# Powers on GpSimd, another lane order, an earlier router chain and spare products in a two-layer network on one core

## The reference, cut to what matters

```python
# retention of layer 2, its end (stage E)
mu = jnp.mean(o, axis=-1, keepdims=True)
var = jnp.var(o, axis=-1, keepdims=True)
o = (o - mu) * jax.lax.rsqrt(var + EPS)
o = jax.nn.silu(g) * o.reshape(b, l, d)
o = o @ Wout
...
# expert layer of layer 1 (stage C)
gate_scores = jax.nn.softmax(gate_logits, axis=-1)
topk_val, topk_idx = jax.lax.top_k(gate_scores, TOP_K)
topk_val = topk_val / (topk_val.sum(axis=-1, keepdims=True) + EPS)
for e in range(E):
    a, b = jnp.split(h, 2, axis=-1)
    g = a * jax.nn.sigmoid(b)
    out = out + eo * comb[..., e:e + 1]
# expert layer of layer 2 (end of stage E)
probs = jax.nn.softmax(logits, axis=-1)
top_w, top_i = jax.lax.top_k(probs, TOP_K)
top_w = top_w / jnp.sum(top_w, axis=-1, keepdims=True)
h = jax.nn.gelu(jnp.einsum('nc,ech->enh', xf, w1), approximate=False)
out = jnp.einsum('ne,enc->nc', comb, y)
```

## Time and profile before

| what | value |
|---|---|
| median of three runs | 281.28 us (279.18 to 285.86) |
| the profiled execution's own time | 281.34 us |
| its span, first to last instruction | 279.6 us |
| mean granted clock of TensorE | 0.933 of full speed |
| busy: TensorE, its weight loads | 235.5 us (84%), 171.5 us (61%) |
| busy: VectorE, ScalarE, GpSimd | 191.2 us (68%), 128.1 us (46%), 43.2 us (15%) |
| the chain that ended last, by engine | TensorE 60%, VectorE 23%, ScalarE 9%, issue 4%, GpSimd 1%, DMA 1% |

### The profile page before, as it was taken

The page is one execution under the profiler, slowest core; times in us unless marked ns, Lnnn a source line. Parts: engine busy times, 40 slices in busy tenths (PEclk is TensorE's granted clock), DMA queues, the critical chain, the costliest instruction groups (busy, mean ns, idle before and its releaser), DMA issues.

```text
span 279.6 us, 4964 instructions
## 1 busy us (share of the span) xinstructions
PE 235.5 (84%) x1885; PEld 171.5 (61%) x1885; DVE 191.2 (68%) x550; ACT 128.1 (46%) x274; POOL 43.2 (15%) x65
## 2 busy tenths in 40 slices
PE   8858676957869679699995998759878999999995
PEld 8445453635434565244592564437666999999995
DVE  6998899587578667979866768785779655424111
ACT  1377785644161106233305955762424564363331
POOL 6000000000100038367320001210350010100000
PEclk9999998695597999999999999986995999999999
DMA  6970000003980300000000000000000000000000
GB/s 179 356 295 1 2 4 0 2 2 83 438 382 1 147 6 0 2 0 0 0 4 1 2 2 1 1 2 0 4 0 0 0 4 0 2 0 19 2 0 19
DMA packets 5564, 13.74 MB, mean 49 GB/s; under 512 B 2081, under 2 KB 3745, under 8 KB 4898
## 3 DMA queue, kind: packets, MB, share of 16 engines
q1 hardware_dynamic: 4096, 10.73, 10.3%
q10 hardware_dynamic: 1442, 2.66, 2.9%
HBM read 13.13 MB, written 0.26 MB: 48 GB/s over the span
## 4 chain that ended last, share of the span: by engine, by line
PE 60%; DVE 23%; ACT 9%; issue 4%; POOL 1%; DMA 1%; DVEq 0%; ACTq 0%
PE BK L2329 11%; PE BK L2344 10%; PE BK L2109 7%; PE BK L2212 3%; PE BK L2185 3%; ACT WTF L750 3%; PE BK L2196 2%; DVE WTF L1370 2%; PE BK L1932 2%; PE BK L2136 2%; DVE WTF L1215 2%; PE BK L1829 2%; PE BK L2058 2%; ACT WTF L821 1%; PE BK L2041 1%
## 5 line engine op out<-in xcount | busy, mean ns | idle before, releaser
L2329 PE MATMUL BK<-XT,WTF 128*128 128x256 f32 x128 | 32.8, 404 | 0.0
L2344 PEld LDWEIGHTS BK<-WTF 128*128 128x128 f32 x256 | 30.9, 192 | 0.8
L906 ACT ACTIVATE WTF<-BK 128x512 f32<-128x512 f32 x32 | 18.9, 598 | 26.4 <-PE BK L2329 26.4
L2344 PE MATMUL BK<-WTF 128*128 128x128 f32 x256 | 31.0, 275 | 0.0
L2109 PE MATMUL BK<-XT,WTF 128*128 128x512 f32 x64 | 28.7, 594 | 0.0
L2329 PEld LDWEIGHTS BK<-XT,WTF 128*128 128x128 f32 x128 | 25.0, 205 | 3.2
L1724 DVE SCALAR_TENSOR_TENSOR X<-BK,CW,X 128x128 f32<-128x128 f32 x32 | 9.7, 346 | 24.7 <-PE BK L2344 24.7
L750 ACT ACTIVATE WTF<-BK 128x512 f32<-128x512 f32 x40 | 22.6, 601 | 7.1 <-PE BK L1915 7.0
L597 POOL TENSOR_TENSOR RSTD<-VE,MHALF 128x2 f32<-128x2 f32 x8 | 5.6, 710 | 103.9 <-DVE VE L1043 103.1
L821 ACT ACTIVATE WTF<-BK,MN 128x128 f32<-128x128 f32 x64 | 18.0, 394 | 6.7 <-DVE MN L1469 6.7
L2109 PEld LDWEIGHTS BK<-XT,WTF 128*128 128x128 f32 x64 | 12.0, 190 | 14.1 <-issue 12.8
(11 more groups left out here) (309 smaller groups left out, 457.7 us busy)
## 6 DMA issues: line engine op xcount, KB each, us to landing
WTF<-w_f_dram SPq DMA_DIRECT2D x2, 2048.0 KB, 14.5
WTF<-w_c_dram SPq DMA_DIRECT2D x1, 2048.0 KB, 7.7
decay<-c_decay_dram ACTq DMA_DIRECT2D x1, 1024.0 KB, 7.3
decay<-mask_q_dram SPq DMA_DIRECT2D x1, 1024.0 KB, 4.8
crows_sb<-c_rows_dram ACTq DMA_DIRECT2D x1, 544.0 KB, 8.1
w_e_sb<-w_e_dram SPq DMA_DIRECT2D x1, 480.0 KB, 4.8
w_b_sb<-w_b_dram SPq DMA_DIRECT2D x1, 384.0 KB, 5.5
WTF<-win_dram SPq DMA_DIRECT2D x1, 320.0 KB, 6.2
```

The source lines that it names most:

```text
L906: act.activation(GT[:, e % 2, 2 * p:2 * p + 2, lane_cols(h)], lane_bank(h, 2 + p).rearrange("p (a n) -> p a n", a=2), ACT.Gelu).then_inc(e ...
L2329: ins = pe.matmul(lane_bank(h, 2 + p)[:, 256 * i:256 * i + 256], w_f1[:, o:o + P], XT[:, lane_cols(h)], start=True, stop=True)
L2344: ins = pe.matmul(lane_bank(h, e % 2)[:, i * P:(i + 1) * P], GT[:, e % 2, j, b * P:(b + 1) * P], w, start=(j == 0), stop=(j == 3))
```

## The change

It has five parts.
- `deviation(h)` and `route(h)` leave ScalarE for GpSimd. The deviation is the power -1/2 of 128x32 numbers, which VectorE has scaled before; the reciprocal behind it goes. The route is the power of e (a new tile `EBASE`) with 16 columns. ScalarE has a Gelu of one column after `square(0)`.
- GpSimd's keys and values of stage D are made in stage B, as `last_values()` and `last_keys()`. Its bias and residual of stage C stand behind the sums of experts.
- In stage C, `up(2)` is cut in halves, of which the first stands between the transposes of the shares and `widen_share(0)`; `widen_share(1)` follows at once. The last expert's shares and products are taken in halves.
- The orders of stage E are changed on all four engines. TensorE takes lane 0's context between the two halves of `values(3)`, `ff_up(0)` ahead of lane 1's transposes, `ff_down(0)` ahead of `project_qkvg(1)`, and lane 1's context one expert later.
- `stay_warm` is put at ten more kinds of places, with counts of their own, and two waits that stood ahead now stand behind it.

```diff
--- before.py
+++ after.py
@@ GpSimd
+            pool.memset(EBASE[:, :], float(np.e))
...
-            def keys_and_values():
-                pool.wait_ge(b_o_ps, 4)
+            def last_values():
+                pool.wait_ge(a_ctx, 4)
+                settle(pool.memset(VMD, 0.0))
+                settle(pool.memset(ONEH[:, :, :], 0.0))
+                pool.memset(own(ONEH[:, :, :]), 1.0).then_inc(d_blk, 1)
+                pool.wait_ge(vd_ready, 1)
+                pool.tensor_copy(own(VMD), vd[:, :, :].rearrange("p b (g j d) -> p (b g) j d", g=4, j=4))\
+                    .then_inc(d_blk, 1)
+
+            def last_keys():
+                pool.wait_ge(b_s_ps, 16)
                 pool.wait_ge(kd_ready, 1)
                 for b in range(B):
                     pool.tensor_tensor(QB[:, 0, 4 * b:4 * b + 4, :], kTd[:, b, :].unsqueeze(1).to_broadcast([P, 4, P]),
                                        head[:, :].unsqueeze(2).to_broadcast([P, 4, P]), ALU.mult).then_inc(d_blk, 1)
...
                 if s == "B":
                     power(LN_B)
                     pool.memset(CW3[:, :, :, :], 0.0).then_inc(consts_ready, 1)
+                    last_values()
+                    last_keys()
                 if s == "C":
                     power(LN_C)
-                    pool.wait_ge(ln_xhat, xhat_count(LN_C))
-                    keys_and_values()
...
+                    def deviation(h):
+                        pool.wait_ge(l_vs, h + 1)
+                        pair = lane_pair(h)
+                        pool.tensor_tensor(SM2[:, pair, :], SM1[:, pair, :], MHALF[:, 0:1].unsqueeze(2).to_broadcast([P, 2, H]),
+                                           ALU.pow).then_inc(std_ready, 1)
+                    def route(h):
+                        pool.wait_ge(r_z, 2 + h)
+                        pair = lane_pair(h)
+                        pool.tensor_tensor(EX[:, pair, :], EBASE[:, 0:1].unsqueeze(2).to_broadcast([P, 2, NE]), EX[:, pair, :],
+                                           ALU.pow).then_inc(r_exp, 1)
                     lane_power(LN_E, 0)
                     rotate(0)
+                    deviation(0)
                     lane_power(LN_E2, 0)
                     lane_power(LN_E, 1)
                     bypass(0)
+                    lane_power(LN_F, 0)
                     rotate(1)
-                    lane_power(LN_F, 0)
+                    route(0)
+                    deviation(1)
                     lane_power(LN_E2, 1)
                     bypass(1)
                     lane_power(LN_F, 1)
+                    route(1)
@@ ScalarE, stage E
                     square(0)
-                    deviation(0)
+                    act.activation(VM[:, :], col("eps"), ACT.Gelu)
                     context(0)
                     second_xT(0)
+                    gate_ff(0, (0, 1))
                     gate_xT(1)
-                    gate_ff(0)
+                    gate_ff(0, (2,))
                     take_qkvg(1)
+                    last_xT(0)
                     between(1)
...
@@ VectorE
-                        dve.tensor_reduce(m1, hv(OQ), AX.X, ALU.add).then_inc(l_vs, 1)
+                        settle(dve.tensor_reduce(m1, hv(OQ), AX.X, ALU.add))
+                        dve.tensor_scalar(m1, m1, 4.0 / HD, 4.0 * EPS, ALU.mult, ALU.add).then_inc(l_vs, 1)
...
-                        settle(dve.reciprocal(m1, m2))
-                        dve.tensor_tensor(hv(CT), hv(OO), over(m1, HD, 2), ALU.mult).then_inc(ctx_ready, 1)
+                        dve.tensor_tensor(hv(CT), hv(OO), over(m2, HD, 2), ALU.mult).then_inc(ctx_ready, 1)
... (the order after contexts(0))
+                    attended(0)
                     divide(3)
-                    attended(0)
+                    lane_norm(LN_E2, 0, CT)
                     looked_up(1)
                     first_stats(1)
-                    lane_norm(LN_E2, 0, CT)
                     lane_norm(LN_E, 1, X)
+                    gated_ff(0, (0,))
                     convolve(1)
+                    gated_ff(0, (1,))
                     gated_xT(1)
-                    gated_ff(0)
+                    gated_ff(0, (2,))
+                    finished(0)
                     gated_q(1)
-                    finished(0)
+                    lane_norm(LN_F, 0, X)
                     choices(1)
+                    chances(0)
                     shares(1)
-                    lane_norm(LN_F, 0, X)
                     gate_out(1)
+                    best_two(0)
+                    weigh(0, 0)
                     weights(1)
-                    chances(0)
+                    weigh(0, 1)
                     outputs(1)
-                    best_two(0)
                     centred(1)
+                    weigh(0, 2)
+                    variances(1)
                     bypass(1)
-                    variances(1)
-                    weigh(0, 0)
                     contexts(1)
-                    weigh(0, 1)
-                    weigh(0, 2)
+                    weigh(0, 3)
                     attended(1)
...
@@ TensorE, stage A
                         if k == 0 and a == 0:
+                            if g in (1, 3):
+                                stay_warm((0, 1, 2, 7)[u % 4], 5 + g)
                             pe.wait_ge(a_r, g + 1)
...
-                        if i == 0:
-                            pe.wait_ge(a_w, NK * v + NK)
...
+                        if i == 0:
+                            if v in (0, 5, 7):
+                                stay_warm(sample_bank(n), 8 if v == 5 else 5)
+                            pe.wait_ge(a_w, NK * v + NK)
@@ TensorE, stage B
-                        pe.wait_ge(b_pt, 4 * b + 4)
                         if b >= 2:
                             pe.wait_ge(b_sq, b - 1)
+                        if b == 3:
+                            stay_warm(6 + b % 2, 8)
+                        pe.wait_ge(b_pt, 4 * b + 4)
...
                     scores(0)
+                    stay_warm(5, 6)
@@ TensorE, stage C
-                    stay_warm(3)
+                    stay_warm(3, 11)
                     norm_T(LN_C, 7)
+                    stay_warm(3, 4)
...
                     ins.then_inc(c_wide_ps, 1)
+                    up(2, (0, 1))
                     pe.wait_ge(c_split, 1)
                     widen_share(0)
-                    for e in range(1, NE):
+                    widen_share(1)
+                    up(2, (2, 3))
+                    for e in range(2, NE - 1):
                         widen_share(e)
-                        if e + 1 < NE:
-                            up(e + 1)
+                        up(e + 1, (0, 1) if e == NE - 2 else range(4))
+                    widen_share(NE - 1)
+                    up(NE - 1, (2, 3))
@@ TensorE, stages D and E
-                    stay_warm(1)
+                    stay_warm(1, 10)
...
                     scores(range(0, 4))
+                    stay_warm(2, 10)
...
                     turn(13)
+                    stay_warm(5, 4)
                     turn(14)
+                    stay_warm(5, 4)
                     turn(15)
-                    values(3)
+                    stay_warm(5, 3)
+                    values(3, (0,))
                     turn_context(0)
+                    stay_warm(6, 4)
                     project_context(0)
+                    values(3, (1,))
+                    stay_warm(6, 6)
                     project_keys(1)
-                    stay_warm(3, 8)
                     lane_norm_T(LN_E2, 0, 1)
+                    stay_warm(6, 4)
+                    ff_up(0)
                     lane_norm_T(LN_E, 1, 1)
-                    ff_up(0)
+                    stay_warm(6, 4)
+                    ff_down(0)
                     project_qkvg(1)
-                    ff_down(0)
-                    stay_warm(3)
+                    stay_warm(6, 8)
                     lane_norm_T(LN_F, 0, 0)
...
                     up(0, 3)
+                    down(0, 2)
+                    up(0, 4)
                     turn_context(1)
-                    down(0, 2)
+                    down(0, 3)
                     project_context(1)
...
```

86 lines of the change are left out of this document (38 added, 48 removed).

## The result

The changed kernel takes 292.44 us (median of 4 runs, 290.05 to 295.72) against 281.33 for the kernel before beside it: ratio 1.039, interval 1.029 to 1.050, so slower. The forecast was 274.4, its range 270.5 to 283.5, and "slower" had a chance of 0.10.

A forecast was written before the change was run, and what follows sets the result against it. TensorE was taken to bound the kernel, busy 84% of the span with its clock dipping to 0.50. Terms -1.7, -0.8, -2.4, +0.1, -3.1 gave -7.9, plus 1.0 unplaced: 281.34 - 6.9 = 274.4 us, range 270.5 to 283.5.

The forecast's parts named there:

- T: Time of one 32-column power on GpSimd, taken as 1.4 us, with ends of 0.7 and 7.8.
- Rival 1: Power dear per column, waits at lane 0's context and `turn_context(1)`: 271.6 + 2T us, up to 290; chance 0.24.
- the 1.0 us set aside: Added to the sum for what no row places: two held VectorE instructions, or a clock falling in lane 1's new wait.
- lane 0's context: Stage E: context rows ready at 191.15 us, and TensorE takes them at once instead of at 192.12: -1.0 us.
- lane 1's context: Stage E, `turn_context(1)`: a new TensorE wait of about 1.0 + 1.4 us opens, +2.4 us.
- Lane 0 to the experts: Stage E, from lane 0's context to `up(0, 0)`: four pieces sum to 17.95 us instead of 19.9, -1.95 us.
- Stage B: Spare products hold the clock, -1.0, and cost +0.2; GpSimd's new work costs 0, up to 1 uncovered: -0.8 us.
- rival 3: Powers on GpSimd hold VectorE's second read on lane 1's choices, gate and comparisons: 275.9 us; chance 0.08.
- Stage A: Spare products bring unit 5's samples to full clock, 2.2 us gained, 0.5 lost at the first units: -1.7 us.
- Stage C: Router chain without GpSimd contention; TensorE's waits of 1.89 and 0.69 us go: -2.4 us, bounds 0 and 2.6.
- Stage D: Ten spare products ahead of the first transposes, which wait for the exponentials: +0.1 us.
- Rival 2: The clock falls as often as before, only elsewhere; gains in stages A, B and E are lost: 280.2 us; chance 0.10.

The follow-up runs named there:

- kernel 1: The changed kernel with the two deviations back on ScalarE, routes still powers on GpSimd: 279.58 us, 0.993 of before.
- 3: The kernel before with only deviations and routes as powers on GpSimd, plus the early Gelu activation: 290.67 us, 1.030 of before.
- kernel 6: The changed kernel with `gelu(0, 3)` ahead of `square(1)` on ScalarE: 292.39 us, 1.034 of before.
- 11: The changed kernel with deviations on ScalarE, early Sqrt and Gelu, later memsets, gelu before square, 14 and 8 more spare products: 274.12 us, 0.978 of before.
- kernel 13: 12 with memsets behind stage B's second norm, early Sqrt and Gelu, 8 spare products behind `back(7)`; old stage E order: 274.50 us, 0.977 of before.
- Kernel 14: 11 run again unchanged, on the same chip as kernel 13: 274.04 us, 0.976 of before.
- kernel 4: The changed kernel with GpSimd's two memsets for the last values held until stage B's second norm is done: 287.50 us, 1.022 of before.
- kernel 2: The changed kernel with both deviations and routes back on ScalarE: 285.29 us, 1.014 of before.
- 12: The kernel before with the change's edits to stages A to D, plus routes as powers on GpSimd: 279.38 us, 0.987 of before.
- kernel 16: The kernel before with only the change's spare products of stages A to D: 280.71 us, 0.985 of before.
- 5: The changed kernel without the spare products ahead of stage A's first units; those at units 5 and 7 stay: 291.68 us, 1.032 of before.
- kernel 7: The changed kernel without any of the spare products that the change adds: 299.10 us, 1.059 of before.
- kernel 15: The kernel before with the router chain edits alone, memsets held behind stage B's second norm: 279.74 us, 0.996 of before.

## Why the prediction was wrong

**The power (the step that failed).** "I let each further column cost about 0.02 us, ten times a product's." It costs 0.16. T is 5.53 and not 1.4, the route 2.90 and not 1.0. The bound at the far end, all per column, gave 7.8 and 4.0: the truth lies nearer to it, and the row of 2 columns could not tell. The reason given, that fixed parts are usual, was no row of this case. Kernels 1 and 3 show it from both sides: 12.9 us less by the medians without the two deviations, 9.95 us more (290.67 to 280.72 on its chip) with the powers alone. Rival 1 had the place, both waits and the formula, 271.6 + 2 x 5.53 = 282.7, "plus some 3 us of slow clock"; it had 0.24 and should have had the larger part.

**What the power does not explain.** The profiled execution is 15.6 us above the forecast. T, twice, is 8.3 of them. With the right T alone the forecast would have been 282.7, inside its own range. The other 7.4 us are stages A and B (2.8), lane 0 from its context to the experts (2.7) and what lies behind `up(0, 0)` (2.9, most of it clock); stages C and D cancel, and the 1.0 us set aside comes off. Kernel 1 shows that much of this hangs on the power too, through the clock: without the deviations it is 12.9 us faster and not 8.3.

**Its two waits.** At lane 0's context +3.18 instead of -1.0: the difference, 4.18, is T's error of 4.13. At lane 1's context the forecast was 1.0 + T, which is 6.5 with the T measured; it is 1.95 + 4.25 = 6.2 us. The 1.95 us at `up(0, 4)`, behind `square(1)`, was not foreseen and, by kernel 6, cost nothing: the next wait takes over what it gives back.

**The clock behind them.** The forecast had named "a clock that falls in the new wait" and put it and more at 1.0. Behind lane 1's context a `down`, the projection and an `up` take 3.62 + 1.06 + 2.39 us, in kernel 1 1.95 + 0.61 + 1.89: 2.6 us there alone.

**Lane 0 to the experts.** -1.95 forecast, +0.72 measured. In pieces as forecast: 5.72 us (4.4; in kernels 1 and 11, where the clock holds, 4.41), 8.50 (7.65), 3.97 (3.85), 2.44 (2.05). One piece was the clock again, one mis-sized by 0.85. In kernel 1, at full clock, it is 19.32 us: the gain is 0.6 there and not 1.95. And that gain comes from the clock and not from the order: up to the logits kernel 1 takes 18.85 us and the old order at full clock 18.68 (kernel 13). The new order by itself gives nothing here, and the equal times of 13 and 14 agree for the whole. Kernel 14's 19.69 against kernel 1's 18.85 says that 14 more products are too many for a wait of 2.03 us; fewer were not tried.

**Stage B, cover that failed.** The forecast wrote "the fills of the values; nothing waits for it before stage D". The keys were placed well, and the decay products run back to back as forecast. The fills lie over a norm, and 1.6 us go on the path (kernel 4), more than the "up to 1" allowed if the cover failed. Contention as in rival 3, but by an instruction that only writes, and in the stage whose cover I had not looked at.

**Stage A.** -1.7 forecast. The samples did run at full clock and the first products did cost 1.06 us, above the bound of 1.0 and never absorbed up to unit 5. By the last samples it was -1.2, and 0.8 of it went at the branch: the wait there is 0.31 us before, 0.82 to 1.12 in six kernels that have stage A's spare products and 2.20 to 3.33 in four more that have them (1, 2, 12 and 16), and none in 11, 13 and 14, where 8 products run meanwhile. It is 0.30 and 0.44 in kernels 5 and 7, which lack the first or all of these products. What sets it stays open.

**Stage C was right**, -2.78 for -2.4 (the clock is 1.00 in both). It is worth less as a time, 1.2 us in kernel 15: there the clock falls in the next stage, which has no added spare products. It also falls there in kernel 7, but not in the kernel before, so that the missing products are the cause is likely and not shown. Stage D: +0.45 for +0.1.

**Spare products as a whole.** The forecast's clock terms come to some 6 us of gain (2.2, 1.0, 2.6); kernel 7 puts them at 6.7 in the changed kernel, so their size was about right there. On the kernel before, those of stages A to D alone are not shown to give anything (kernel 16). Rival 2, the clock that falls elsewhere, came true in part: behind the powers' waits, and between stages A and B, where nothing was put, as the rival says. From 73.90 to 80.50 the granted clock is 0.54, in the kernel before 0.75.

**Sums.** Two are off by about 0.1 us and change nothing: 189.2 and 0.42 are given as 189.75, and lane 1's parts come to 6.0 and not 6.1.

**The rule on table loads.** The forecast set a drain of 1.38 us (the Trainium skill, ScalarE: Activation LUTs, section What ACT_TABLE_LOAD costs) against the trace's 0.02. No run here shows that drain: in kernel 2 a load of 1.28 us makes a wait of 1.09 us on TensorE, not 2.4. The rule for exp and sqrt that the prediction cites (the Trainium skill, ScalarE: Activation LUTs, section Rules for kernel authors: ScalarE is the only option) fell for exp of 16 columns, which kernel 1 has on GpSimd and which is faster there than on ScalarE (kernel 2). For the root of 32 columns GpSimd can do it too, but is far slower.

## What to carry to other kernels

Where the change stands on an operation at a size that no row shows, take the fixed and the per-element cost from two sizes; with one size, the far end deserves as much chance as the near one, and its price counts once for every wait that it is in. A wait on TensorE can cost more than its length, as the products behind it may run at the lower clock (2.6 us here behind the second context); kernels 1 and 2 have the same wait of 2.03 us, one with the clock held behind it and one without. Moving work to an idle engine also moves it over other instructions: look at what runs beside it, memsets included, and check that a stage's gain is still there a stage later.

## What was not expected of the hardware

- A power on GpSimd: 0.70, 2.90 and 5.53 us for 2, 16 and 32 columns of 128 partitions.
- A VectorE product of one fp32 SBUF input with two columns of scalars, 0.30 us, is held by a GpSimd memset of 1.81 us beside it (2.23 us for two). VectorE's products of two inputs in the router's chain are not held by the same memset: in the kernel before, 0.43 and 0.42 us beside it (107.95 to 109.75), and after, without it, 0.42. The Trainium skill, SBUF — State Buffer, section Who interferes with whom, has a `tensor_scalar` in a two-port mode contend with GpSimd, and an instruction with two SBUF inputs only with a GpSimd instruction that reads; the traces agree with both.
- TensorE's wait at a branch on a flag is between 0.82 and 3.33 us in kernels whose stage A is the same (4 and 1), and no wait is left with 8 spare products ahead of the branch (11, 13, 14).
- The fastest kernel of the case is 14 (and 11): 274.04 us, 0.976 of before, with the deviations on ScalarE, their tables early, the routes on GpSimd, the memsets behind the norm and TensorE's waits filled. Kernel 13, in the old order, is within 0.5 us of it.
